# Graph attention layer on one core: score weights' products first, two load queues in the head, and 1/deviation moved into the transposes' matrix

## The chip, the cores and the metric

The kernel runs on one core of a Trainium2 chip. The metric is the device time of one execution in microseconds (us). Lower is better. Five engines work side by side, each through its own list of instructions in order: TensorE (PE, matmuls), VectorE (DVE), ScalarE (ACT), GpSimd (POOL) and SyncE (SP, which here only starts transfers). They wait for each other through semaphores.

## The reference

There are 2048 nodes with 256 features each. Cut to what matters:

```python
h0 = maximum(layernorm(x), 0.0)                      # (x - mean) / sqrt(var + 1e-5)
type_sum = adj @ h0
attn_a = sigmoid(concat([type_sum, h0]) @ Wa.T + ba)
attn_b = sigmoid(concat([type_sum, h0]) @ Wb.T + bb)
h = h0 @ W_sa
scores = (h @ a_left)[:, None] + (h @ a_right)[None, :]
e = where(adj != 0, exp(-leaky_relu(scores, 0.01)), 0.0)
x_a = (e / (e.sum(1, keepdims=True) + 1e-5)) @ h
x_b = adj @ (h0 @ W_gcnb) + b_gcnb
out = x + sigmoid(attn_a * x_a + attn_b * x_b)
```

`adj` is a 2048x2048 matrix of zeros and ones.

## The kernel before, in words

The nodes are 16 tiles of 128 (NT), taken in 8 pairs; the columns of the adjacency are four chunks of 512 (NC). Each float32 matrix is split into a high and a low float16 part (`_hi`, `_lo`), and a product is three matmuls: high by high, high by low, low by high.

The order of every engine is written out by hand. The work has these stages:

- **Head.** Units of one tile (0 and 1) or two tiles (2 to 8) go through `moments` (DVE: mean and variance), `norms` (POOL: 1/deviation by a power, `rstd`, then the shift), `h0_tiles` (ACT: the normalized, clipped tile in place in `x_sb`, counted by `h0_done`), `nat_highs` and `nat_lows` (the float16 parts of h0), `turn` (PE: transposes in float32 by the identity), `h0t_highs` and `h0t_lows` (the parts of the transposed tile) and `wide` (PE: h0 times the 260 wide columns, that is W_sa, two gate columns, and two score columns; the weights of the last two are products of W_sa and the attention vector, made at L926 from `c_sb`). Units 6 to 8 (tiles 10 to 15) are transposed by DMA instead (`turn_by_dma`, three times two transfers on SP's queue). `warm` runs matmuls on zeros.
- **b products** (`b_pair`, `b_products`, L822): h0 parts times the adjacency, chunk by chunk. Chunks 0, 1 and 2 come before the attention products of chunk 0, chunk 3 after those. Chunk 0 is interleaved with the head, pair by pair.
- **Attention** (`a_pair`, L863 to L865): DVE and ACT make `e` from the scores (`dve_z`, `act_exp`, `act_high`, `dve_low`), PE multiplies it by the weighted h. `post` (L856) applies the second weight matrix.

The scores of all nodes are needed as a row on every partition. `sl_lines` transposes them on PE, ACT copies them to `c_sb` (L388), SP stores them to memory (`sl_store`, L259) and loads them back broadcast (`sl_spread`, L264). This goes in three parts.

All loads of x and of the weights are on SP's queue. The adjacency is loaded by POOL (`load_adj`, L305) in 12 pieces, `ADJ_PIECES`: pieces 0 to 5 are chunk 0 (the first four with two tiles each), 6 and 7 chunk 1, 8 and 9 chunk 2. POOL starts piece 8 only when all six DMA transposes have landed (the loop at L337), and SP starts nothing out of its order. x is loaded in 7 parts, `X_PARTS`; below x5 is the part with tiles 8 to 11 and x6 that with tiles 12 to 15.

## Time and profile before

| | |
|---|---|
| time, median of 3 runs | 177.93 us (177.76 to 178.66) |
| the profiled execution, own time | 176.94 us |
| its span (first to last instruction) | 175.1 us |
| PE busy | 170.5 us, 97% of the span |
| DVE busy | 144.5 us, 83% |
| ACT busy | 113.2 us, 65% |
| POOL busy | 24.5 us, 14% |
| chain of work that ended last: PE's share | 97% |

The rows below come from that one execution; times within it count from the span's start. Outside the span lie 1.84 us of its own time. The busy time of PE includes the matmuls on zeros.

### The profile page before, as it was taken

The page shows a single profiled execution, that of the slowest core. Times are in us where ns is not written, and L with a number is a line of the kernel's source. Part 1 is how long each engine was busy: PE and PEld are TensorE (multiplying, and loading weights), DVE is VectorE, ACT ScalarE, POOL GpSimd, SP SyncE. Part 2 cuts the span into 40 slices and gives each one's busy share as a digit, 9 for nine tenths or more (in the row PEclk, how much of TensorE's full clock was granted, in tenths as well). Part 3 has the DMA queues.
Part 4 walks back from the last instruction along what each step waited for, and adds up shares of the span by engine and source line. Part 5 has one row for each costly group of instructions (what it writes and reads, how often), then busy time and mean ns, then how long its engine had stood idle before and what let it go on. Part 6 is the DMA issues. An engine that isn't in the chain of part 4 may idle for free.

```text
span 175.1 us, 3378 instructions
## 1 busy us (share of the span) xinstructions
PE 170.5 (97%) x1313; PEld 124.6 (71%) x1313; DVE 144.5 (83%) x306; ACT 113.2 (65%) x167; POOL 24.5 (14%) x43
## 2 busy tenths in 40 slices
PE   7999999999999999999999999999999999999992
PEld 2556764455554478888744488888888888888892
DVE  3799995589999995999999703999999999976551
ACT  3769996349868889298658600875875874863310
POOL 4846441002007930000000000000000000000000
PEclk9999999999999999999999999999999999999998
DMA  5999999986999369900010100000010010011101
GB/s 135 296 213 260 226 231 175 207 157 110 215 220 332 146 112 216 247 28 2 0 64 0 60 0 0 4 0 0 4 60 0 6 60 0 4 62 60 64 30 30
DMA packets 9071, 17.66 MB, mean 101 GB/s; under 512 B 3920, under 2 KB 4704, under 8 KB 8288
## 3 DMA queue, kind: packets, MB, share of 16 engines
q0 software_dynamic: 1728, 8.39, 25.0%
q1 hardware_dynamic: 7328, 9.06, 16.3%
q8 instruction: 10, 0.16, 0.4%
q14 instruction: 5, 0.04, 0.1%
HBM read 22.94 MB, written 2.11 MB: 143 GB/s over the span
## 4 chain that ended last, share of the span: by engine, by line
PE 97%; DVE 1%; issue 0%; ACT 0%; DVEq 0%
PE ps L822 32%; PE ps L865 16%; PE ps L863 16%; PE ps L864 16%; PE ps L856 6%; PE ps L797 6%; PE ps L905 3%; PE ps L791 1%; PE ps L926 0%; DVE logit L771 0%; DVE e_lo L557 0%; PE ps L818 0%; ACT logit L434 0%; DVE res L664 0%; DVE e_hi L519 0%
## 5 line engine op out<-in xcount | busy, mean ns | idle before, releaser
L863 PE MATMUL ps<-mv_lo,e_hi 128*128 128x257 f16 (+2 forms) x272 | 71.0, 267 | 0.0
L865 PE MATMUL ps<-mv_hi,e_lo 128*128 128x257 f16 (+2 forms) x272 | 70.9, 266 | 0.0
L864 PE MATMUL ps<-mv_hi,e_hi 128*128 128x257 f16 (+2 forms) x272 | 70.8, 266 | 0.0
L400 ACT ACTIVATE z<-z,log_e 128x1024 f32<-128x1024 f32 x32 | 36.7, 1146 | 31.2 <-DVE z L601 31.2
L601 DVE SCALAR_TENSOR_TENSOR z<-sl_row,exs,far 128x512 f32<-128x512 f32 x64 | 45.1, 746 | 0.6 <-DMA sl_row<-sl_line 0.6
L609 DVE TENSOR_TENSOR e_lo<-z,e_hi 128x1024 f16<-128x1024 f32 x32 | 39.0, 1220 | 1.4 <-ACT e_hi L410 1.4
L822 PE MATMUL ps<-adj,nat_lo 128*128 128x512 f16 x128 | 36.8, 379 | 0.0
L822 PE MATMUL ps<-adj,nat_hi 128*128 128x512 f16 x128 | 36.7, 379 | 0.0
L410 ACT ACTIVATE e_hi<-z 128x1024 f16<-128x1024 f32 x32 | 33.3, 1041 | 0.0
L863 PEld LDWEIGHTS ps<-mv_lo,e_hi 128*128 128x128 f16 x272 | 26.4, 97 | 3.4 <-ACT c_sb L388 0.3
L864 PEld LDWEIGHTS ps<-mv_hi,e_hi 128*128 128x128 f16 x272 | 26.5, 98 | 3.1
L865 PEld LDWEIGHTS ps<-mv_hi,e_lo 128*128 128x128 f16 x272 | 26.4, 97 | 3.1
L822 PEld LDWEIGHTS ps<-adj,nat_lo 128*128 128x128 f16 x128 | 12.5, 98 | 15.1
L822 PEld LDWEIGHTS ps<-adj,nat_hi 128*128 128x128 f16 x128 | 12.5, 98 | 13.1
L588 DVE TENSOR_SCALAR far<-adj 128x1024 f16<-128x1024 f16 x32 | 13.4, 421 | 0.2
L434 ACT ACTIVATE logit<-logit 128x512 f32<-128x512 f32 (+2 forms) x10 | 5.4, 537 | 9.3 <-DVE logit L651 5.3
L363 ACT ACTIVATE x_sb<-x_sb,shift,rstd 128x256 f32<-128x256 f32 x16 | 8.8, 590 | 3.3 <-POOL shift L312 3.3
L618 DVE SCALAR_TENSOR_TENSOR gate_in<-ps,gate_c 128x4 f32<-128x4 f32 x8 | 1.3, 157 | 10.5 <-PE ps L856 10.5
L305 POOL DMA_DIRECT2D adj<-in_adj_t x12 | 7.1, 591 | 16.0 <-DMA e_lo<-nat_lo 14.2
L856 PE MATMUL ps<-wg_hi,agg_hi 128*128 128x258 f16 x32 | 8.8, 274 | 0.0
L856 PE MATMUL ps<-wg_hi,agg_lo 128*128 128x258 f16 x32 | 8.7, 273 | 0.0
L856 PE MATMUL ps<-wg_lo,agg_hi 128*128 128x258 f16 x32 | 8.7, 272 | 0.0
(69 smaller groups left out, 170.0 us busy)
## 6 DMA issues: line engine op xcount, KB each, us to landing
adj<-in_adj_t POOLq DMA_DIRECT2D x6, 1024.0 KB, 9.8
x_sb<-in_x SPq DMA_DIRECT2D x6, 512.0 KB, 8.2
out<-res SPq DMA_DIRECT2D x7, 256.0 KB, 2.0
adj<-in_adj_t POOLq DMA_DIRECT2D x4, 256.0 KB, 6.7
adj<-in_adj_t POOLq DMA_DIRECT2D x2, 512.0 KB, 8.7
x_sb<-in_x SPq DMA_DIRECT2D x3, 256.0 KB, 4.0
sl_row<-sl_line SPq DMA_DIRECT2D x2, 256.0 KB, 5.5
sl_row<-sl_line SPq DMA_DIRECT2D x1, 512.0 KB, 7.0
```

The source lines that it names most:

```text
L363: act.activation(x_sb[:, t, :], x_sb[:, t, :], ACT.Relu, bias=shift[:, t:t + 1], scale=rstd[:, t:t + 1]).then_inc(h0_done, 1)
L400: act.activation(z[:, n % ZRING, :, :], z[:, n % ZRING, :, :], ACT.Exp, bias=log_e[:, 0:1], scale=SLOPE - 1.0).then_inc(exp_done, 1)
L410: act.activation(e_hi[:, s:s + 2, :], z[:, n % ZRING, :, :], ACT.Copy).then_inc(e_high, 1)
L588: dve.tensor_scalar(far[:, n % 2, :, :], adj16[:, c % ADJ, j:j + 2, :], -FAR, FAR, ALU.mult, ALU.add)\
L601: ins = dve.scalar_tensor_tensor(out=z[:, n % ZRING, u, :], in0=sl_row[:, c * CW:(c + 1) * CW], scalar=exs[:, j + u, SR:SR + 1], in1=far[: ...
L609: dve.tensor_tensor(e_lo[:, s:s + 2, :], z[:, n % ZRING, :, :], e_hi[:, s:s + 2, :], ALU.subtract)\
L797: ins = pe.matmul(ps[:, wide_bank(t), cols], h0t[a][:, t, k, :], wa2[b][:, k, cols], start=((a, b) == (0, 0) and k == 0), stop=(a == 1 and ...
L822: ins = pe.matmul(ps[:, B_BANKS[c] + k, :], nat[h][:, j, k * P:(k + 1) * P], adj16[:, c % ADJ, j, :], start=(j == 0 and h == 0), stop=(j = ...
L856: ins = pe.matmul(ps[:, 6 + q, 0:WG], agg[a][:, c % AGG, k, cols], wg2[b][:, k, :], start=(i == 0), stop=(i == len(three) - 1))
L863: pe.matmul(ps[:, bank, cols], e_hi[:, s, i1], mv_lo[:, j, cols], start=(j == 0), stop=False)
L864: pe.matmul(ps[:, bank, cols], e_hi[:, s, i1], mv_hi[:, j, cols], start=False, stop=False)
L865: return pe.matmul(ps[:, bank, cols], e_lo[:, s, i1], mv_hi[:, j, cols], start=False, stop=(j == NT - 1))
```

## The change

In PE's list the four small products of the score weights (L926 before, L1006 after) come ahead of all transposes. The first two tiles are only centred and clipped by ACT (`centred`), and their transposes become ordinary float32 matmuls whose second matrix is the identity times 1/deviation (`turn_scaled`, with `diagonal` on DVE); their float16 parts are scaled by `rstd` (`first_nat_highs`, `first_nat_lows`). The low parts of the first two tiles' wide products are put behind b products. Of matmuls on zeros, 12 become 6. `c_sb` and `wa_sb` are loaded from ACT's queue and no longer from SP's; `wg_sb` and `r_sb` are loaded after adjacency piece 8 has landed; x6 is started when x5 has landed; adjacency pieces 3 to 6 are each started behind one more unit's `norms`. From unit 4 on POOL makes two small operations that DVE made. ACT's order in the head is written out anew, with h0 halves ahead of evictions, and `wide` of units 3 to 5 comes later among the b products.

```diff
-WARM = 7
+WARM = 5
...
-SL_UNITS = (3, 5)
-SL_BANKS = (6, 6, 0)
+SL_UNIT = 3
+SL_BANKS = (6, 3, 0)
...
-WIDE_BANKS = (6, 2, 6, 2, 6, 2, 0, 2)
+
+POOL_FROM = 4
+
+NCENTRED = 2
+WIDE_BANKS = (6, 2, 6, 2, 0, 2, 0, 2)
...
+        diag = res[:, 0, :, 0:P]
...
-            sp.dma_start(wa_sb[:, :, :], w_wide).then_inc(wa_landed, 16)
-            sp.dma_start(c_sb[:, :], consts).then_inc(c_landed, 16)
             load_x(3)
             sp.wait_ge(x_landed[2], 16)
             load_x(4)
             sp.wait_ge(x_landed[3], 16)
             load_x(5)
-            sp.wait_ge(adj_landed[1], 16)
+            sp.wait_ge(x_landed[5], 16)
             load_x(6)
-            sp.wait_ge(x_landed[6], 16)
-            sp.dma_start(wg_sb[:, :, :], w_post).then_inc(wg_landed, 16)
-            sp.dma_start(r_sb[:, :], rows).then_inc(rows_landed, 16)
...
             sl_store(0)
+            sp.wait_ge(adj_landed[piece_of(1, 0)], 16)
             sl_spread(0)
-            sp.wait_ge(adj_landed[piece_of(0, NT - 1)], 16)
             turn_by_dma(ONTIME)
             turn_by_dma(ONTIME + 1)
             sl_store(1)
             turn_by_dma(ONTIME + 2)
             sl_spread(1)
             sp.wait_ge(adj_landed[piece_of(2, 0)], 16)
+            sp.dma_start(wg_sb[:, :, :], w_post).then_inc(wg_landed, 16)
+            sp.dma_start(r_sb[:, :], rows).then_inc(rows_landed, 16)
...
-                pool.wait_ge(var_ready, u + 1)
+                if u < POOL_FROM:
+                    pool.wait_ge(var_ready, u + 1)
+                else:
+                    pool.wait_ge(moments_done, UNITS[u][1])
+                    pool.tensor_scalar(var_s[:, ts], mean_var[:, ts, 1], LN_EPS, H_SCALE ** -2, ALU.add, ALU.mult).then_inc(var_ready, 1)
+                    pool.tensor_scalar(neg_mean[:, ts], mean_var[:, ts, 0], -1.0, None, ALU.mult).then_inc(neg_ready, 1)
+                    pool.wait_ge(var_ready, u + 1)
                 pool.tensor_tensor(rstd[:, ts], var_s[:, ts], power[:, 0:UNITS[u][1] - UNITS[u][0]], ALU.pow).then_inc(rstd_ready, 1)
+                if u < NCENTRED:
+                    return
                 pool.wait_ge(rstd_ready, u + 1)
+                if u >= POOL_FROM:
+                    pool.wait_ge(neg_ready, u + 1 - POOL_FROM)
+                if u < POOL_FROM:
+                    pool.wait_ge(centre_ready, u + 1)
                 pool.tensor_tensor(shift[:, ts], neg_mean[:, ts], rstd[:, ts], ALU.mult).then_inc(norm_ready, 1)
...
+            norms(3)
             load_adj(3)
-            norms(3)
+            norms(4)
             load_adj(4)
-            norms(4)
+            norms(5)
             load_adj(5)
-            norms(5)
+            norms(6)
             load_adj(6)
-            norms(6)
...
+            def centred(u):
+                act.wait_ge(centre_ready, u + 1)
+                act.activation(x_sb[:, u, :], x_sb[:, u, :], ACT.Relu, bias=neg_mean[:, u:u + 1], scale=1.0).then_inc(h0_done, 1)
+
             def h0_tiles(u):
...
+            def first_nat_highs():
+                act.wait_ge(h0_done, NCENTRED)
+                act.wait_ge(rstd_ready, NCENTRED)
+                for t in range(NCENTRED):
+                    ins = act.activation(nat_hi[:, t, :], x_sb[:, t, :], ACT.Copy, scale=rstd[:, t:t + 1])
+                ins.then_inc(nat_high, 1)
+
+            def w_wide_high():
+                act.wait_ge(wa_landed, 16)
+                act.activation(wa_hi[:, :, 0:WG], wa_sb[:, :, :], ACT.Copy, scale=W_SCALE).then_inc(wa_high, 1)
...
+            act.wait_ge(ident_ready, 1)
+            act.dma_start(c_sb[:, :], consts).then_inc(c_landed, 16)
+            act.dma_start(wa_sb[:, :, :], w_wide).then_inc(wa_landed, 16)
             act.wait_ge(consts_ready, 1)
             act.activation(table[:, :], log_e[:, :], ACT.Exp)
-            h0_tiles(0)
-            h0_tiles(1)
+            centred(0)
+            w_wide_high()
+            centred(1)
             h0t_highs(0)
+            first_nat_highs()
             h0t_highs(1)
             h0_tiles(2)
-            nat_highs(0)
             nat_highs(1)
             h0t_highs(2)
             h0_tiles(3)
+            nat_highs(2)
+            h0_tiles(4)
+            h0t_highs(3)
+            nat_highs(3)
             mv_highs(0)
-            nat_highs(2)
-            for p in range(1, NPAIR):
-                if p + 2 < NTURN:
-                    h0t_highs(p + 2)
-                if p + 2 < NPAIR:
-                    h0_tiles(p + 3)
-                    nat_highs(p + 2)
-                if p < ONTIME - 1:
-                    mv_highs(p)
-            mv_highs(ONTIME - 1)
+            mv_highs(1)
+            h0_tiles(5)
+            h0t_highs(4)
+            nat_highs(4)
+            h0_tiles(6)
+            nat_highs(5)
+            h0_tiles(7)
+            nat_highs(6)
+            h0t_highs(5)
+            mv_highs(2)
+            h0_tiles(8)
+            nat_highs(7)
+            mv_highs(3)
+            mv_highs(4)
             agg_highs(0)
-            act.wait_ge(wg_landed, 16)
-            act.activation(wg_hi[:, :, :], wg_sb[:, :, :], ACT.Copy, scale=W_SCALE).then_inc(wg_high, 1)
+            sl_lines(1)
...
+            def diagonal(u):
+                if u == 0:
+                    dve.wait_ge(ident_ready, 3)
+                dve.wait_ge(rstd_ready, u + 1)
+                dve.tensor_scalar(diag[:, u, :], ident[:, :], rstd[:, u:u + 1], None, ALU.mult).then_inc(diag_ready, 1)
+
+            def w_wide_low():
...
+            def turn_scaled(u):
+                pe.wait_ge(diag_ready, u + 1)
+                pe.wait_ge(h0_done, u + 1)
+                for k in range(KT):
+                    ins = pe.matmul(turn_bank(u)[:, 0, k, :], x_sb[:, u, k * P:(k + 1) * P], diag[:, u, :], start=True, stop=True)
+                ins.then_inc(turned, 1)
...
             warm(WARM)
-            pe.wait_ge(stats_done, 1)
-            warm(1)
-            pe.wait_ge(var_ready, 1)
-            warm(2)
-            pe.wait_ge(norm_ready, 1)
-            warm(1)
-            pe.wait_ge(ident_ready, 3)
-            turn(0)
-            warm(1)
-            turn(1)
-            pe.wait_ge(wa_high, 1)
-            pe.wait_ge(h0t_high, 1)
-            wide_part(0, slice(0, WG), ((0, 0),))
             pe.wait_ge(c_landed, 16)
             for k in range(KT):
                 for m in range(KT):
                     ins = pe.matmul(wl_bank[:, k, :], wt_sb[:, m, k * P:(k + 1) * P],
                                     c_sb[:, C_AVEC + 2 * m:C_AVEC + 2 * m + 2], start=(m == 0), stop=(m == KT - 1))
             ins.then_inc(wl_product, 1)
-            pe.wait_ge(wa_low, 1)
-            wide_part(0, slice(0, WG), ((0, 1),))
+            warm(1)
+            turn_scaled(0)
+            turn_scaled(1)
+            pe.wait_ge(wa_high, 1)
+            pe.wait_ge(wa_ready, 1)
+            for t in range(NCENTRED):
+                pe.wait_ge(h0t_high, t + 1)
+                wide_part(t, slice(0, WA), ((0, 0),))
+                pe.wait_ge(wa_low, 1)
+                wide_part(t, slice(0, WA), ((0, 1),))
+            b_pair(0)
+            turn(2)
             pe.wait_ge(h0t_ready, 1)
-            wide_part(0, slice(0, WG), ((1, 0),))
-            wide(1)
-            wide_part(0, slice(WG, WA)).then_inc(wide_product, 1)
-            turn(2)
-            b_pair(0)
-            for p in range(1, NPAIR):
-                b_pair(p)
-                if p + 2 < NTURN:
-                    turn(p + 2)
-                if p + 1 < NTURN:
-                    wide(p + 1)
-            b_products(1, 0, 8)
+            wide_part(0, slice(0, WA), ((1, 0),)).then_inc(wide_product, 1)
+            b_pair(1)
+            turn(3)
+            wide_part(1, slice(0, WA), ((1, 0),)).then_inc(wide_product, 1)
+            wide(2)
+            b_half_pair(2, 0)
+            turn(4)
+            b_half_pair(2, 1)
+            b_pair(3)
+            turn(5)
+            wide(3)
+            b_pair(4)
+            b_pair(5)
+            b_pair(6)
+            wide(4)
+            wide(5)
+            b_pair(7)
+            b_products(1, 0, 3)
+            pe.wait_ge(mv_ready, 8)
+            sl_lines(1)
+            b_products(1, 3, 8)
+            pe.wait_ge(sl_moved, 2)
             wide(6)
             b_products(1, 8, 12)
             pe.wait_ge(h0t_ready, NTURN)
```

The first place is PE's head, before the change (`e_hi` under 128x512 is the zeros tile, `c_sb` the score weights' products, `ident,x_sb` the transposes, `wa_*` the wide products, `adj,nat_*` the b products of chunk 0, from the first on):

```order
L905 MATMUL ps<-e_hi 128x512 x11
L791 MATMUL ps<-ident,x_sb 128x128 x2
L905 MATMUL ps<-e_hi 128x512
L791 MATMUL ps<-ident,x_sb 128x128 x2
L797 MATMUL ps<-wa_hi,e_hi 128x258 x2
L926 MATMUL ps<-c_sb 128x2 x4
L797 MATMUL ps<-wa_lo,e_hi 128x258 x2
L797 MATMUL ps<-wa_hi,e_lo 128x258 x2
L797 MATMUL ps<-wa_hi,e_hi 128x260 x2
L797 MATMUL ps<-wa_lo,e_hi 128x260 x2
L797 MATMUL ps<-wa_hi,e_lo 128x260 x2
L797 MATMUL ps<-wa_hi,e_hi 128x2 x2
```

and with the change (`res,x_sb` are the scaled transposes of the first two tiles):

```order
L998 MATMUL ps<-e_hi 128x512 x5
L1006 MATMUL ps<-c_sb 128x2 x4
L998 MATMUL ps<-e_hi 128x512
L882 MATMUL ps<-res,x_sb 128x128 x4
L888 MATMUL ps<-wa_hi,e_hi 128x260 x2
L888 MATMUL ps<-wa_lo,e_hi 128x260 x2
L888 MATMUL ps<-wa_hi,e_hi 128x260 x2
L888 MATMUL ps<-wa_lo,e_hi 128x260 x2
L911 MATMUL ps<-adj,nat_hi 128x512 x4
L911 MATMUL ps<-adj,nat_lo 128x512 x4
L875 MATMUL ps<-ident,x_sb 128x128 x4
L888 MATMUL ps<-wa_hi,e_lo 128x260 x2
```

The score weights' products moved from behind the first wide product to the front, and the b products of chunk 0 now start ahead of the third unit's transposes (the row under the b products) and of the first low products.

The second place is ACT around the first copy of the score lines (`c_sb<-ps 4x128`), before the change:

```order
L363 ACTIVATE x_sb<-x_sb,shift,rstd 128x256 x2
L373 ACTIVATE nat_hi<-x_sb 128x512
L379 ACTIVATE scale_a<-exs,log_s 128x2
L383 ACTIVATE mv_hi<-ps,scale_a 128x256 x2
L368 ACTIVATE e_hi<-ps 128x512
L363 ACTIVATE x_sb<-x_sb,shift,rstd 128x256 x2
L373 ACTIVATE nat_hi<-x_sb 128x512
L388 ACTIVATE c_sb<-ps 4x128
```

and with the change, from the evictions of the second pair's wide products on:

```order
L412 ACTIVATE scale_a<-exs,log_s 128x2
L416 ACTIVATE mv_hi<-ps,scale_a 128x256 x2
L385 ACTIVATE x_sb<-x_sb,shift,rstd 128x256 x2
L390 ACTIVATE e_hi<-ps 128x512
L406 ACTIVATE nat_hi<-x_sb 128x512
L385 ACTIVATE x_sb<-x_sb,shift,rstd 128x256 x2
L406 ACTIVATE nat_hi<-x_sb 128x512
L385 ACTIVATE x_sb<-x_sb,shift,rstd 128x256 x2
L406 ACTIVATE nat_hi<-x_sb 128x512
L390 ACTIVATE e_hi<-ps 128x512
L421 ACTIVATE c_sb<-ps 4x128
```

The copy stood behind the half of the fifth pair (the fifth `nat_hi` row of ACT), and stands now behind that of the seventh pair, which needs x6.

The third place is SP's queue up to the first DMA transpose, before the change:

```order
L239 DMA x_sb<-in_x 128x256 x2
L239 DMA x_sb<-in_x 128x512
L244 DMA wa_sb<-in_w_wide 128x516
L245 DMA c_sb<-in_consts 128x516
L239 DMA x_sb<-in_x 128x512 x2
L239 DMA x_sb<-in_x 128x1024 x2
L254 DMA wg_sb<-in_w_post 128x516
L255 DMA r_sb<-in_rows 128x258
L259 DMA sl_line<-c_sb 4x128
L264 DMA sl_row<-sl_line 128x512
L270 DMA_TRANSPOSE e_hi<-nat_hi 128x4x128
```

and with the change:

```order
L248 DMA x_sb<-in_x 128x256 x2
L248 DMA x_sb<-in_x 128x512 x3
L248 DMA x_sb<-in_x 128x1024 x2
L263 DMA sl_line<-c_sb 4x128
L268 DMA sl_row<-sl_line 128x512
L274 DMA_TRANSPOSE e_hi<-nat_hi 128x4x128
```

Four loads left the queue ahead of the store of the score lines (`sl_line`); its spread (`sl_row`) and the six transposes still follow it in order.

## Rows read from the trace of the kernel before

**Rows 1.** The page, part 2: 40 slices of 4.4 us; clock and DMA share in tenths.

```profile
PEclk9999999999999999999999999999999999999998
DMA  5999999986999369900010100000010010011101
```

**Rows 2.** Waits of PE over the whole span: total us, times, longest us.

```profile
PE ps L905 <- DVE e_hi L519: 1.2, 1, 1.2
PE ps L797 <- DVE e_lo L557: 0.3, 1, 0.3
```

**Rows 3.** Timeline of PE, 1 to 16 us: start us, length us, engine, line, operation, count.

```profile
1.18 4.88 PE L905 MATMUL ps<-e_hi 128*128 128x512 f16 x11 [1.18 <-DVE e_hi L519]
5.84 0.63 PE L791 MATMUL ps<-ident,x_sb 128*128 128x128 f32 x2
6.27 0.63 PE L905 MATMUL ps<-e_hi 128*128 128x512 f16 x1
...
7.26 0.95 PE L926 MATMUL ps<-c_sb 128*128 128x2 f32 x8
...
9.83 0.64 PE L791 MATMUL ps<-ident,x_sb 128*128 128x128 f32 x4
10.30 1.03 PE L822 MATMUL ps<-adj,nat_hi 128*128 128x512 f16 x4
...
14.42 0.38 PE L797 MATMUL ps<-wa_lo,e_hi 128*128 128x260 f16 x2
...
15.54 0.81 PE L822 MATMUL ps<-adj,nat_hi 128*128 128x512 f16 x3
```

**Rows 4.** Timeline of POOL and ACT, 3.9 to 5 us.

```profile
3.97 0.60 POOL L310 TENSOR_TENSOR rstd<-var_s,power 128x1 f32<-128x1 f32 x1
...
4.64 0.19 POOL L312 TENSOR_TENSOR shift<-neg_mean,rstd 128x1 f32<-128x1 f32 x1
...
4.87 0.60 ACT L363 ACTIVATE x_sb<-x_sb,shift,rstd 128x256 f32<-128x256 f32 x1 [2.65 <-POOL shift L312]
```

**Rows 5.** Line L305 from 3 to 5 us: adjacency piece 0, issue and us to landing.

```profile
L305 POOL DMA_DIRECT2D adj<-in_adj_t x1: 707/707/707, 3.2 to 3.2; - x1
...
DMA to landing us min/median/max: 5.5/5.5/5.5
```

**Rows 6.** Line L239 from 7 to 9 us: x5, issue and us to landing.

```profile
L239 SPq DMA_DIRECT2D x_sb<-in_x x1: 328/328/328, 7.1 to 7.1; - x1
...
DMA to landing us min/median/max: 7.4/7.4/7.4
```

**Rows 7.** Line L239 from 10 to 12 us: x6, issue and us to landing.

```profile
L239 SPq DMA_DIRECT2D x_sb<-in_x x1: 328/328/328, 10.7 to 10.7; - x1
...
DMA to landing us min/median/max: 8.7/8.7/8.7
```

**Rows 8.** Timeline, 21.7 to 26.5 us: unit 7's statistics and the seventh pair's high half.

```profile
21.81 0.74 DVE L527 BATCH_NORM_STATS2 stats<-x_sb 128x6 f32<-128x256 f32 x2
...
25.81 0.63 ACT L373 ACTIVATE nat_hi<-x_sb 128x512 f16<-128x512 f32 x1
```

**Rows 9.** Timeline of SP: the score lines' store and spread, first and last DMA transpose.

```profile
21.25 0.37 SPq L259 DMA_DIRECT2D sl_line<-c_sb  x1
27.99 0.35 SPq L264 DMA_DIRECT2D sl_row<-sl_line  x1
28.45 1.31 SPq L270 DMA_TRANSPOSE e_hi<-nat_hi  x1
...
37.20 2.15 SPq L270 DMA_TRANSPOSE e_lo<-nat_lo  x1
```

**Rows 10.** Line L305 at 41 us: adjacency piece 8, issue and us to landing.

```profile
L305 POOL DMA_DIRECT2D adj<-in_adj_t x1: 530/530/530, 41.0 to 41.0; - x1
...
DMA to landing us min/median/max: 7.5/7.5/7.5
```

**Rows 11.** Timeline of PE from 48.5 us: the first b products of chunk 2.

```profile
48.85 0.59 PE L822 MATMUL ps<-adj,nat_hi 128*128 128x512 f16 x2
```

129 lines of the change are left out of this document (81 added, 48 removed).

## The prediction

> **What bounds the kernel now.** I read the page first, then the waits, then the timelines of the places that the change touches. The list of PE's waits has two lines: 1.2 us before anything can start and 0.3 us in the head, for a low part of a transposed tile [rows 2]. From there to the end of its work PE never stands still, so a gain can only come from the head, before about 9 us, or from less work on PE. A loss can come from anywhere PE is made to wait. The page also shows what could make it wait: the DMA engines are full through the first eight slices, 0 to 35 us, while the clock row says full speed throughout [rows 1]. The clock row is not to be taken literally at the start: 11 matmuls of 512 columns on zeros took 4.88 us, 0.44 us each, which is 1.2 GHz, while from 10.30 us on four b products of 512 columns take 1.03 us with their overlapping tail, under 0.26 us each, which is 2.4 GHz [rows 3]. PE worked without a gap from 1.18 us until the clock had risen.
>
> **Accounting for the head.** I take the point at which the third b pair starts, 15.54 us before [rows 3]. From the first b product (10.30) to there PE does two b pairs, one set of transposes and one two-tile wide product: 5.24 us. With the change the same stretch holds two things more, because they now come behind the first b pair: the four transposes of unit 2 (9.83 to 10.30, 0.47 us [rows 3]) and the low products of tiles 0 and 1, four matmuls of 260 columns at 0.11 us (two start within 0.22 us at 14.42 [rows 3]), 0.45 us. With S for the new start of the first b pair, the third pair starts at S + 6.16. It is earlier than before only if S is below 9.38. The gain is 9.38 - S.
>
> **What sets S.** Removed: POOL's shift from the chain of the first tile. Before, `rstd` runs from 3.97 to 4.57, the shift from 4.64 to 4.83, ACT's tile starts at 4.87 and takes 0.60 us [rows 4], and the transposes follow at 5.84 [rows 3]. With the change ACT centres the tile while POOL makes the power, and DVE scales the identity afterwards. That operation is not in the trace; it costs between nothing and the 0.60 us of ACT's tile, which has twice the elements, and I take 0.2. The matrix is then ready near 4.9 instead of the tile at 5.5, if x lands as before. It will not quite: `c_sb` now travels beside x on ACT's queue, with twice its bytes and more; I allow 0 to 0.6 us of delay for x0 and take 0.4, my choice. So the first transposes start at about 5.3, half a us earlier. The four score weights' products (0.95 us as eight records [rows 3]) move into time in which PE ran zeros, which costs nothing. Dropping six matmuls on zeros costs nothing by itself either.
>
> ACT then has, in order, the halving of `wa_sb` (which must land first), the second tile's centring, one eviction of 256 columns, two scaled halves and a second eviction. At 0.4 to 0.6 us each (a tile takes 0.60 [rows 4], a two-tile half 0.63 [rows 8]) from about 5.5 this ends near 8.2, and the first b pair could start at 8.6 to 9.0. But adjacency piece 0 is not earlier: it is issued when x0 has landed (3.2 us) and takes 5.5 us, so 8.7 [rows 5], and with x0 0.3 to 0.4 later about 9.0. I take S = 9.2, bounds 8.4 and 10.0. The head gives 0.18 us, bounds +1.0 and -0.6.
>
> The scaled transposes are plain float32 matmuls of 128 columns, which the trace does not have. The nearest rows are the float32 products of two columns, 0.95 us for four, and the transposes, 0.43 us for two at the low clock (5.84 to 6.27) [rows 3]. I take 0.85 us for a tile's two, bounds 0.43 (no dearer than the transposes) and 1.9 (all four products' time twice). The page "TensorE: Matmul & The Clock Gate" of the Trainium skill, in its section "Terms", gives the transpose mode as four times faster for FP32, which speaks against this edit: it would make each pair of scaled transposes 1.7 us at the low clock. No run here shows it yet.
>
> **Clock.** The new list leaves gaps: after five matmuls on zeros PE is idle from 3.4 us (five at 0.44 from 1.18) until `c_sb` lands, which I put at 4.1,, and again around each scaled transpose. Before, it had none until the clock rose. If the rise comes after S, each us of real work until then costs half a us extra per us of time, so 0 to 1.3 us; I take 0.4.
>
> So PE comes to the first b product of chunk 2, 48.85 before [rows 11], at 48.85 - 0.18 + 0.4 = 49.1, if nothing in between stops it. POOL's ten added small operations are of the shift's kind, 0.19 us [rows 4], and take ten as small from DVE; they lie beside PE's work, and without that cover would cost 1.9 us.
>
> **What else gets later.** Moved weights first: `wg_sb` and `r_sb` no longer go ahead of the store of the score lines, and are needed by the first `post` only, amid the attention products of chunk 0. But x6 is started later. Before it was issued at 10.7 and landed 8.7 us later, 19.4 [rows 7], right behind x5, which landed at 14.5 (7.1 and 7.4) [rows 6]. Now it is issued when x5 has landed. I take x5 at 13.5, since adjacency piece 2 is started later and leaves room. From x5's landing x6 took 4.9 us although it was queued; unqueued it takes 4.9 to 8.7, I take 6.0: x6 at 19.5.
>
> From x6 the chain of unit 7 leads to the seventh pair's high half, from 21.81 (DVE) to 26.44 (end of ACT's half), 4.63 us before [rows 8]. ACT's copy of the score lines now stands behind this half and one eviction. With 0.6 and 0.25 for these, less 0.5 for time that ACT was merely busy, the store of the score lines is issued at 24.5; before it was at 21.25 [rows 9]. SP then waits for the store before it issues the spread: 6.74 us before (27.99), with two loads ahead [rows 9]. I take 4.5 now (bounds 3 and 6.7): the spread at 29.0. Behind it in SP's order are all six DMA transposes, the last issued at 37.20 for 2.15 us [rows 9], and behind them POOL's adjacency piece 8, issued at 41.0 and landing 7.5 us later, 48.5 [rows 10]. PE takes its first product from it at 48.85 [rows 11]. This is the thin place of the kernel: 0.3 us of slack. From spread to issue it was 13.0 us. The transposes' issues took 1.31 us at first and 2.15 at last; with the bulk loads done earlier I take 0.8 off: 12.2, bounds 10.5 and 13.0. Piece 8 is issued at 41.2 and lands at 48.8.
>
> **Sum.** The end moves by the later of the two, PE at 49.1 and the data at 48.8, against 48.85: +0.2 us. The own time of the profiled execution goes from 176.94 to 177.15. The median of the runs shown is 177.93, 0.99 above it, so I forecast 178.15 on that scale.
>
> The other rule that speaks against this is on the page "DMA: Bandwidth & Descriptors", section "Queues, rings and completion order" of the Trainium skill: each DMA engine takes turns between queues by packet. A second queue in the head then slows x0 rather than only adding a path, and small stores take turns with long adjacency packets. Here the first shows only as the allowance above.
>
> **The rivals.** (1) *The store chain decides, slower.* x6 at 20.3, the store at 25.3, 5 us to the spread, 12.7 and 7.5 us from there: piece 8 lands at 50.5, and PE waits. That is +1.65 us, 179.6 (own 178.6). It decides once piece 8 is issued after 41.3. For it: every step is in order on one queue and the slack was 0.3. Against it: `wg_sb` and `r_sb` are out of the way. Bound: x6 at 22.2, 6.7 and 13.0 give 54.4, +5.5; I do not believe all of them together. (2) *The clock rises late, slower.* Two us of real work behind S at 1.2 GHz: PE at 48.85 - 0.18 + 1.2, +1.0 us, 178.95. (3) *The head gains and nothing is lost behind.* S = 8.4 and a clock that has risen: -1.0 us, 176.95. It needs piece 0 before 8.4 and piece 8 before 47.9. Piece 0's 5.5 us speak against it. (4) *Scaled transposes at four times the transposes' time*, 4 x 0.43 = 1.7 us a tile at the low clock: the two tiles take 1.7 us more than I took, of which 0.9 lies beside ACT's work, so S is 10.0 and PE is busy enough for the clock: +0.6, 178.55, still no measurable change. This is what the page "TensorE: Matmul & The Clock Gate" of the Trainium skill would give. (5) The change doing nothing is inside my forecast: x0's delay cancels the earlier transposes.
>
> **How the numbers follow.** A measurement of this kernel can tell about 0.5%, 0.9 us. Forecast within 0.9 us: 0.40, and rival 4, 0.10, beside it: same 0.50. Rival 1 has 0.25 and rival 2 has 0.10: slower 0.35. Rival 3 has 0.15: faster. The forecast's own range is 177.2 to 178.8. The whole range goes down to rival 3, 176.9, and up past rival 1 to 180.2, which leaves out half of rival 3 and the tail of rival 1's bound.
>
> **What would show each step.** Right: the first b product at about 9.2; x0's statistics 0.3 to 0.5 later than before; piece 0 landing near 9.0; x6 landing at 19 to 20; the store of the score lines issued after 24; piece 8 issued near 41.2; PE without a wait above 0.3 us between 10 and 49 us. Wrong for the head: the first b product before 8.6 or after 10. Wrong for the chain: the store issued before 22, or PE waiting for an adjacency piece elsewhere, such as piece 1, 2 or 3, whose uses come 0 to 1.5 us earlier. Wrong altogether: PE waits in the middle of chunk 0 for x6's halves (it needs the seventh pair at S + 15.4 = 24.6, and 19.5 + 4.6 is 24.1), which would add up to 1 us ahead of the thin place and be hidden by rival 1 if that holds.

## The result and the profile after

The changed kernel takes 180.53 us (median of 22 runs, 178.21 to 184.20), the kernel before 177.31 us in the same sessions (22 runs, 176.62 to 178.66). The ratio is 1.011, 95% interval 1.008 to 1.014: slower, by less than 2%, with an interval clear of 1. This ratio and those below leave out every run more than 1.5% above the fastest of its kernel, which takes out ten of the changed kernel's 22 runs and none of the other's, while every median in us is over all runs (180.53 is 1.8% above 177.31). The spread grew as well.

The profiled execution of the changed kernel took 179.12 us (span 177.3), 2.2 more than that of before, and 1.4 less than its own median. What follows is read from it. First PE's waits over the whole span (total us, times, longest us), against two lines in [rows 2]:

```profile
PE ps L911 <- DMA adj<-in_adj_t: 1.5, 1, 1.5
PE ps L998 <- DVE e_hi L565: 1.2, 1, 1.2
PE ps L1006 <- DMA c_sb<-in_consts: 0.6, 1, 0.6
PE ps L911 <- DVE nat_lo L629: 0.2, 1, 0.2
```

There is a new wait for adjacency, and it has one place. PE's timeline around chunk 2's first b product, first a line of before (the product itself started at 48.85 [rows 11]), then of after:

```profile
48.62 0.38 PE L797 MATMUL ps<-wa_hi,e_lo 128*128 128x260 f16 x2
```

```profile
49.16 0.38 PE L888 MATMUL ps<-wa_hi,e_lo 128*128 128x260 f16 x2
51.04 0.59 PE L911 MATMUL ps<-adj,nat_hi 128*128 128x512 f16 x2 [1.50 <-DMA adj<-in_adj_t]
```

PE sat idle from 49.54 and started at 51.04, 2.19 us later than before, and its last product ends 2.19 us later too (174.15 against 171.96). So everything that was lost was lost before 51 us. The idle time tells a little less than the stop: records overlap, the next one started 0.23 us after such a row before (48.62 to 48.85), so without the wait the product would have started at about 49.39. The stop is 1.65 us, and every idle time below is about 0.15 short in the same way. The head (against [rows 3]):

```profile
1.18 2.32 PE L998 MATMUL ps<-e_hi 128*128 128x512 f16 x5 [1.18 <-DVE e_hi L565]
4.06 1.87 PE L1006 MATMUL ps<-c_sb 128*128 128x2 f32 x8 [0.56 <-DMA c_sb<-in_consts]
...
6.17 1.96 PE L882 MATMUL ps<-res,x_sb 128*128 128x128 f32 x8
7.91 0.64 PE L888 MATMUL ps<-wa_hi,e_hi 128*128 128x260 f16 x2
...
9.48 1.02 PE L911 MATMUL ps<-adj,nat_hi 128*128 128x512 f16 x4
10.35 1.03 PE L911 MATMUL ps<-adj,nat_lo 128*128 128x512 f16 x4
11.21 0.60 PE L875 MATMUL ps<-ident,x_sb 128*128 128x128 f32 x4
11.64 0.39 PE L888 MATMUL ps<-wa_hi,e_lo 128*128 128x260 f16 x2
11.87 1.02 PE L911 MATMUL ps<-adj,nat_hi 128*128 128x512 f16 x4
13.06 1.04 PE L911 MATMUL ps<-adj,nat_lo 128*128 128x512 f16 x4 [0.17 <-DVE nat_lo L629]
...
14.37 0.39 PE L888 MATMUL ps<-wa_hi,e_lo 128*128 128x260 f16 x2
```

The first b product is at 9.48, 0.82 us earlier than before, but the score weights' products alone now take 1.87 us where they took 0.95: PE runs at 1.2 GHz until 9.29 (until 6.91 before, and the 0.95 came after it). And PE's work from the first b product to chunk 2, busy time over those stretches, first of before, then of after (window, length, busy, matmul records, granted clock, DMA share, GB/s):

```profile
10.30:48.85 38.55, 38.55 (x229) 1.00 0.95 198
```

```profile
9.48:49.54 40.06, 39.89 (x236) 1.00 0.96 179
```

The busy time grew by 1.34 us, but not all of that is moved work. The rows that moved behind the first b product are unit 2's transposes (11.21 to 11.64, 0.43 us) and the two pairs of low products (0.23 us each, 11.64 to 11.87 and again at 14.37): 0.89 us. The rest is the two stops, whose first 0.15 us count as busy, and 0.13 us by which unit 5's transposes at 19.83 last longer than the other sets. So the head alone is about even, and the waits are the loss: -0.82 + 0.89 (moved work) + 0.13 + 0.33 (the low half at 13.06, a stop of 0.33 us by the distance of the starts) + 1.65 (piece 8) = 2.18 of the 2.19 us.

Where piece 8 was held is told by the chain that ended last, from 17 to 52 us in order of time (start us, us, what):

```profile
19.86 10.90 DMA adj<-in_adj_t
30.76 0.02 issue
30.78 0.35 SPq L268
...
31.17 2.30 SPq L274
...
39.35 2.98 DMA e_lo<-nat_lo
...
42.36 0.04 POOLq L356
42.41 0.49 issue
42.90 8.00 DMA adj<-in_adj_t
50.90 0.14 issue
51.04 1.02 PE ps L911 x4
```

Piece 6 of the adjacency lands at 30.76, that releases the spread of the score lines (27.99 before [rows 9]), behind it go the six DMA transposes, the last lands at 42.34, and that releases piece 8 (42.90; 41.0 before [rows 10]). ScalarE's timeline and SP's waits show a second thing at the same gate:

```profile
23.73 0.63 ACT L406 ACTIVATE nat_hi<-x_sb 128x512 f16<-128x512 f32 x1
24.27 0.58 ACT L390 ACTIVATE e_hi<-ps 128x512 f16<-128x512 f32 x1
24.74 0.25 ACT L421 ACTIVATE c_sb<-ps 4x128 f32<-4x128 f32 x1
```

```profile
SPq L266 <- DMA sl_line<-c_sb: 3.9, 1, 3.9
...
SPq L268 <- DMA adj<-in_adj_t: 1.5, 1, 1.5
```

The score lines are copied at 24.74, stored at 25.02, and the store has landed at about 29.3 (25.35 + 3.9); only then comes the wait for piece 6. So the spread has two late releasers, 1.5 us apart. In the kernel before, piece 6 (issued at 17.39) landed at 28.22, only 0.23 us after the spread at 27.99: the new wait costs this much because POOL also issues the piece 2.5 us later.

### The profile page after: what moved, and what is told of

Same layout as the page of the kernel before. It is cut to its first block, busy times and chain, and to the rows that moved or that the text cites. A ratio compares the mean times of both kernels' runs of the same rounds, so it can differ in the third digit from the quotient of the medians.

```text
span 177.3 us, 3373 instructions
## 1 busy us (share of the span) xinstructions
PE 170.7 (96%) x1305; PEld 125.6 (71%) x1305; DVE 143.7 (81%) x298; ACT 113.9 (64%) x169; POOL 27.2 (15%) x51
## 3 DMA queue, kind: packets, MB, share of 16 engines
q0 software_dynamic: 1728, 8.39, 25.2%
## 4 chain that ended last, share of the span: by engine, by line
PE 74%; DMA 14%; SPq 5%; POOL 2%; ACT 1%; DVE 1%; issue 1%; POOLq 0%; DVEq 0%
PE ps L911 17%; PE ps L957 16%; PE ps L958 16%; PE ps L956 16%; DMA adj<-in_adj_t 11%; PE ps L949 6%; SPq L274 4%; DMA c_sb<-in_consts 2%; DMA e_lo<-nat_lo 2%; PE ps L1006 1%; PE ps L882 1%; PE ps L888 1%; POOL rstd L322 1%; ACT x_sb L385 1%; POOL shift L330 0%
## 5 line engine op out<-in xcount | busy, mean ns | idle before, releaser
L957 PEld LDWEIGHTS ps<-mv_hi,e_hi 128*128 128x128 f16 x272 | 26.5, 98 | 3.2
L956 PEld LDWEIGHTS ps<-mv_lo,e_hi 128*128 128x128 f16 x272 | 26.4, 97 | 3.3
L958 PEld LDWEIGHTS ps<-mv_hi,e_lo 128*128 128x128 f16 x272 | 26.4, 97 | 3.1
L685 DVE SCALAR_TENSOR_TENSOR gate_in<-ps,gate_c 128x4 f32<-128x4 f32 x8 | 1.3, 157 | 11.2 <-PE ps L949 11.2
L311 POOL DMA_DIRECT2D adj<-in_adj_t x12 | 7.3, 608 | 19.4 <-DMA e_lo<-nat_lo 17.2
L570 DVE BATCH_NORM_STATS2 stats<-x_sb 128x6 f32<-128x256 f32 x16 | 6.2, 417 | 3.0 <-DMA x_sb<-in_x 2.9
## 6 DMA issues: line engine op xcount, KB each, us to landing
adj<-in_adj_t POOLq DMA_DIRECT2D x6, 1024.0 KB, 10.8
```

Of the source, the lines that this page charges most:

```text
L311: pool.dma_start(adj16[:, c % ADJ, lo:hi, :], adj_t[c, :, lo:hi, :]).then_inc(adj_landed[i], 16)
L956: pe.matmul(ps[:, bank, cols], e_hi[:, s, i1], mv_lo[:, j, cols], start=(j == 0), stop=False)
L957: pe.matmul(ps[:, bank, cols], e_hi[:, s, i1], mv_hi[:, j, cols], start=False, stop=False)
L958: return pe.matmul(ps[:, bank, cols], e_lo[:, s, i1], mv_hi[:, j, cols], start=False, stop=(j == NT - 1))
```

## Experiments

Ratios are to the kernel before, measured beside each, with 95% intervals. Times within a run come from one profiled execution of each kernel, which can lie anywhere among its runs: those of e2 and e3 are the fastest and the second fastest of twelve (177.41 and 177.33 us), those of e4 and e5 the slowest of twelve (181.31 and 181.74). Line numbers in the experiments are off by one or two from the changed kernel's.

**e1: the old gate.** Piece 5 is waited for, behind the spread, instead of piece 6 ahead of it.

```diff
             sl_store(0)
-            sp.wait_ge(adj_landed[piece_of(1, 0)], 16)
             sl_spread(0)
+            sp.wait_ge(adj_landed[piece_of(0, NT - 1)], 16)
```

> The changed kernel, only that SP waits for adjacency piece 5, as before the change, and not for piece 6, and does so behind the spread of the score lines instead of ahead of it. Theory A (the new gate on piece 6 decides when the queue behind it starts): the spread is issued at 29.3 us, when the store has landed, instead of 30.8; piece 8 lands at 49.4 instead of 50.9, PE waits for it 0.1 us or less instead of 1.5, and the time falls by 1.4 us against the changed kernel, to within 0.9 us of the kernel before. Rival B (the loads' bandwidth decides, not the gate): the spread goes out earlier but the transposes wait behind piece 7, piece 8 lands within 0.4 us of 50.9 and the time stays. Rival C (the late store decides, behind x6's half on ACT): the store lands only at 30.5 or later in most runs and less than 0.4 us comes back.

Measured: 1.015 (1.010 to 1.021), 180.58 us. The store went at 25.80, the spread at 31.32 when the store had landed, piece 8 at 44.43 to 52.08, and PE waited 2.36 us. The gate alone is not the cause: the store steps into its place. In this profile the clock rose only at 10.81, after the first b product (9.72), and the b products before it started 0.43 us apart instead of 0.22: about 0.5 us.

**e2: POOL's old order.** Pieces 3 to 6 are issued one unit's norms earlier, as before.

```diff
-            norms(3)
             load_adj(3)
-            norms(4)
+            norms(3)
             load_adj(4)
...
```

> The changed kernel with POOL's loads of adjacency pieces 3 to 6 each one unit's norms earlier, as before the change; the gate on piece 6 stays. Theory A (piece 6 is late because POOL issues it late, at 19.9 us instead of 17.4): piece 6 is issued near 17.8 and lands 10.9 us later, near 28.7; the spread then waits for the store, 29.3; piece 8 lands near 49.4 and the time falls by 1.3 to 1.5 us. Rival B (piece 6 is late because the DMA engines are full): issued earlier, it lands after 30 all the same and the time falls by less than 0.4 us. Rival D: earlier adjacency packets slow x5 and x6, the store goes out after 26 us, and the time rises by 0.5 us or more.

Measured: 1.006 (1.002 to 1.010), 179.33 us. Piece 6 was issued at 17.36 and landed at 26.82. Now the store alone holds the spread (25.17, spread 30.39); piece 8 lands at 49.19, and PE waits 0.31 us at 49.33, all in the fastest of its twelve runs. The ratio is about half of the changed kernel's loss, but the two intervals overlap.

**e3: seven products on zeros** (`WARM = 7`).

> The changed kernel with seven matmuls on zeros at its start instead of five, so that PE has no gap before the score weights' products. If piece 8 decides the end alone, the time stays within 0.3 us, whatever the head does. In the trace the clock should rise earlier than 9.3 us (near 7), the first b product should start at 9.0 to 9.2 instead of 9.48, and PE should come to chunk 2 about 0.5 us earlier and wait for piece 8 that much longer (2.0 instead of 1.5 us). The rival is that the head still decides in part: then 0.5 us come back in the time.

Measured: 1.005 (0.999 to 1.010), 179.96 us. In the profile the clock rose at 5.09 and b began at 8.39. PE then waited 0.94 us at 18.11 for piece 3 and came to chunk 2 at 49.25: 1.1 us were gained at the start, and most of it was waited away. What I had not expected: it did not wait for piece 8 at all. With both releasers as in the changed kernel, piece 6 landed at 29.03, the spread went at 29.37 and piece 8 landed at 48.94. So the lateness of that chain is not the same in every execution.

**e4: the loads alone.** The kernel before, with the change's gates, POOL's order, x6 behind x5 and the late `wg_sb` and `r_sb`, and its own head.

```diff
-            sp.wait_ge(adj_landed[1], 16)
+            sp.wait_ge(x_landed[5], 16)
             load_x(6)
-            sp.wait_ge(x_landed[6], 16)
-            sp.dma_start(wg_sb[:, :, :], w_post).then_inc(wg_landed, 16)
...
             sl_store(0)
+            sp.wait_ge(adj_landed[piece_of(1, 0)], 16)
             sl_spread(0)
-            sp.wait_ge(adj_landed[piece_of(0, NT - 1)], 16)
...
```

> The kernel before with the change's load order behind the head alone: SP's gate on piece 6, x6 started when x5 has landed, the post weights loaded after piece 8 and split later, POOL's pieces 3 to 6 each one unit later. Head, ACT's order and the two queues are as before. Theory A: the gate on piece 6 works here too; piece 6 lands near 30.5, the spread goes out then instead of 28.0, piece 8 lands near 50.7 and the time rises by 1.5 to 2.2 us against the kernel before, nearly all of the change's loss. Rival C (ACT's copy behind the seventh half is needed for the loss): the time rises by less than 0.7 us. A further possibility is that PE also waits for x6's halves in chunk 0, which would show as waits before 30 us and not add to the end.

Measured: 1.007 (1.003 to 1.011), 178.89 us. The store left at 19.94, and still the spread waited for piece 6 (issued 20.48, landed 29.86); piece 8 went at 43.08, PE waited 2.62 us. Here piece 6 alone holds the spread, with the store landed long before. The edit has POOL's later issue in it as well, and no run takes the two apart in the old head. This profile is the slowest of its runs, and 1.7 us of it are the clock's (last section).

**e5: the copy early.** ScalarE's copy of the score lines right behind `h0t_highs(4)`. The same edit is in e6 to e9 and in e12.

```diff
-SL_BANKS = (6, 3, 0)
+SL_BANKS = (7, 3, 0)
...
-                if p + 1 == SL_UNIT:
-                    sl_lines(0)
...
             h0t_highs(4)
+            sl_lines(0)
...
-                        pe.wait_ge(mv_ready, t - 3)
+                        pe.wait_ge(mv_ready, max(t - 3, 2))
...
+                    if t == 5:
+                        pe.wait_ge(sl_moved, 1)
```

> The changed kernel, with ScalarE's copy of the first score lines out of PSUM taken right behind h0t_highs(4) instead of inside mv_highs(2) (and in bank 7, so that nothing has to be waited for). Copy at about 20.6 us instead of 24.7, so the store is issued at about 21.1. Theory A (the spread is released by the later of the store's landing and piece 6's landing): piece 6 still lands at 30 to 31 us, so nothing is won: spread at 30 to 31, piece 8 issued at 42 to 43, a wait of 0.8 to 1.8 us before chunk 2, ratio to the kernel before 1.005 to 1.012. Rival B (the store alone decides): spread at 26 to 27, piece 8 lands before 48, no wait, ratio 0.998 to 1.003.

Measured: 1.010 (1.006 to 1.013), 179.89 us. The gate decides: piece 6 landed at 32.79, spread at 32.80, piece 8 at 45.57, PE waited 1.40 us there (in its slowest run, with piece 6 issued 2.5 us later than in the changed kernel's profile). Something else came in: 2.5 us of waiting for piece 1 at 14.75.

**e6: early copy and old gate** (e5 with e1).

> The changed kernel with the early copy and the old gate (spread first, then a wait for piece 5). Theory A: the store is issued at 21.1 and lands at 25.5 to 27, piece 5 has landed at 23, so the spread goes at 25.5 to 27, the six transposes behind it end early enough that piece 8 is issued at 38 to 40.5 and lands by 48; TensorE, arriving at about 49.3, does not wait. Span 175.3 to 176.0, ratio 0.998 to 1.004. Rival C (the head itself, and not the wait, lost the time: clock rise at 9.3 instead of 6.9): no wait and still 1.005 or more. Rival D (the piece-8 chain is bound by piece 7 and POOL's queue, not by the spread): piece 8 issued at 41 or later in spite of a spread at 26.

Measured: 1.008 (1.004 to 1.011), 179.37 us. The store went at 21.40 and the spread at 26.80, four us earlier than in the changed kernel, but piece 8 at 42.85, as late as there. PE waited 0.59 us for piece 3 and 0.63 for piece 8. This is rival D's sign. The six transposes start earlier and end no earlier: from the first one's issue to the last one's landing they took 15.0 us here, 11.2 in the changed kernel and 12.0 before; the second's issue alone took 4.40 us, while piece 7 was in flight. In all the profiles the first transpose landed 0.5 to 2.3 us after piece 7, although it was issued anywhere from 26.4 to 33.2. That piece 7 holds them is likely by this, and no run tests it.

**e7: early copy and POOL's old order** (e5 with e2).

> The changed kernel with the early copy and POOL's loads in the order of before (each piece of 3 to 6 one unit's norms earlier), gate on piece 6 kept. Theory A: piece 6 is issued at 17.4 and lands at 27 to 28.5, which is later than the store (about 26), so the spread goes at 27 to 28.5 as in the kernel before (27.99), piece 8 is issued at 39.5 to 41.2 and lands at 47.5 to 49; wait before chunk 2 none or up to 0.3. Ratio 0.998 to 1.005. Rival C (head lost the time): 1.005 or more without a wait.

Measured: 1.008 (1.005 to 1.012), 179.36 us. The spread went at 27.93, as before, and piece 8 landed at 49.90, before PE asked. PE's waits between 10 and 60 us:

```profile
PE ps L912 <- DMA adj<-in_adj_t: 0.6, 1, 0.6
PE ps L912 <- ACT nat_hi L406: 0.3, 1, 0.3
```

The wait before chunk 2 is gone and the kernel is still 0.8% slower. The reading by that wait alone falls here: PE stops elsewhere. Nor was the chain to piece 8 mended. It landed 1.3 us later than before (48.56), and without its other stops PE would have been there at about 49.1, 0.8 us ahead of it.

**e8: all of these, and seven products on zeros** (e1, e2, e3 and e5 together).

> The changed kernel with the early copy, the old gate, POOL's loads in the old order, and 7 products on zeros instead of 5. Theory A: the chain to piece 8 is early by 1 us or more, and the clock rises at about 5.1 (as it did in the kernel with 7 products), first product of b at 8.4 instead of 9.2 (before: 10.30). TensorE then arrives at chunk 2 at 48.0 to 48.9 and piece 8 has landed at 47.5 to 48.5. Span 174.3 to 175.3, ratio 0.993 to 1.000: the first of these kernels that may beat the kernel before. Rival E (what the head gains is given back at the pieces of adjacency, of which piece 3 then comes too late, by 0.9 us): ratio 0.999 to 1.003, with a wait at piece 3 and first product at 8.4. Rival C: 1.005 or more.

Measured: 1.003 (1.000 to 1.006), 178.30 us, the best of the twelve. The seven products on zeros did not raise the clock early this time: it rose at 9.18 (5.09 in e3), and b began at 9.54. In the profile PE waits after the head for one thing, piece 1. PE's timeline, then line L311 (POOL's adjacency loads) from 6 to 7 us:

```profile
11.70 0.39 PE L887 MATMUL ps<-wa_hi,e_lo 128*128 128x260 f16 x2
13.80 0.38 PE L912 MATMUL ps<-adj,nat_hi 128*128 128x512 f16 x1 [1.72 <-DMA adj<-in_adj_t]
```

```profile
L311 POOL DMA_DIRECT2D adj<-in_adj_t x1: 592/592/592, 6.3 to 6.3; - x1
...
DMA to landing us min/median/max: 7.4/7.4/7.4
```

Piece 1 holds tiles 2 and 3, which is the second b pair. In the kernel before that pair started right behind the first:

```profile
12.03 1.03 PE L822 MATMUL ps<-adj,nat_hi 128*128 128x512 f16 x4
```

So the old head asked for piece 1 at 12.03, when it had been there since 10.7 (issued 5.6, 5.1 us to landing): 1.3 us to spare. The new one asks at 11.0 to 12.7, hardly earlier, but piece 1, issued at 6.1 to 6.4, lands between 10.5 and 14.6. The expectation of e9 has 3.7 us here, from 15.54, which is the third pair and wants piece 2; that is a misreading of mine. Piece 8 landed at 49.64, and without the wait for piece 1 PE would have asked for it at about 49.0.

**e9: x5 held** (e8, with x5 behind piece 0's landing instead of x3's).

```diff
-            sp.wait_ge(x_landed[3], 16)
+            sp.wait_ge(adj_landed[0], 16)
             load_x(5)
```

> The last kernel (early copy, old gate, POOL's old order, 7 products on zeros) with x5 sent behind piece 0's landing (about 8.1 us) instead of behind x3's (6.5). Theory F (in the changed head TensorE asks for piece 1 at 11.8 us, 3.7 us earlier than before, and piece 1, issued at 6.1 to 6.3, lands between 11.7 and 14.6 because x4 and x5 are in flight with it): with x5 held, piece 1 lands by 11.8, no wait there, chunk 2 is reached at 48.6 to 49.2, and ratio 0.994 to 1.001. Rival G (piece 1 is late by x4 and the weights alone): piece 1 still lands at 12.5 to 14, wait of 0.5 to 1.7 there, ratio 1.001 to 1.006. Rival H: x5 is late for its statistics (it would land at 14.5 to 16) and a later pair waits for it.

Measured: 1.014 (1.009 to 1.018), 179.82 us. Piece 1 landed at 10.62, as theory F has it, the clock rose at 4.32, b began at 8.22, and PE paid later on. Its waits from 10 to 50 us:

```profile
PE ps L912 <- DMA adj<-in_adj_t: 1.4, 1, 1.4
PE ps L912 <- DVE nat_lo L628: 1.2, 1, 1.2
PE ps L912 <- ACT nat_hi L406: 0.5, 1, 0.5
```

The first is piece 2 (9.07 to 16.19, beside x5 from 8.00 to 14.32); the others are halves behind x6, which waits for x5 and landed at 22.71. Rival H came in kind, with x6 in the place of x5. What one load gains another loses.

**e10: piece 8 early** (the changed kernel, with piece 8 released by the fourth DMA transpose).

```diff
-            for p in range(ONTIME, NPAIR):
+            for p in range(ONTIME, NPAIR - 1):
                 pool.wait_ge(h0t_landed[p - ONTIME], 32)
             load_adj(8)
+            pool.wait_ge(h0t_landed[NPAIR - 1 - ONTIME], 32)
```

> The changed kernel with one difference: POOL issues piece 8 when the first four transposes by DMA have landed instead of all six (its slot has been free from the start; only the order was held by hand). In the changed kernel the fourth landed at 38.73 and the sixth at 42.34, so piece 8 goes at about 39.3 instead of 42.90 and lands at 47 to 49.5. Theory A (the wait before chunk 2 is a part of the loss, and the head the other): the 1.5 us of waiting go to 0 to 0.3, TensorE reaches chunk 2 at about 49.5, ratio 1.002 to 1.006, 0.5 to 0.8% better than the changed kernel. Rival C (the head alone): the wait goes, and the ratio stays at 1.008 or more. Rival I (the fifth and sixth transpose now come too late for the last wide products, needed at 48.0): a wait at the last wide products in its place, ratio unchanged at 1.009 to 1.012.

Measured: 1.013 (1.009 to 1.018), 179.74 us. The copy was late in this profile (store 27.50, spread 32.58), so piece 8 went at 42.48 all the same and landed at 50.88; PE did not wait for it only because piece 1 (landed 13.56) had already cost it 1.75 us at 13.70.

**e11: the head alone** (the changed kernel with the later loads as before: e1, e2, x6 behind piece 1, `wg_sb` and `r_sb` early; `c_sb` and `wa_sb` stay on ACT's queue).

> The changed kernel with the loads as before (x6 behind piece 1, POOL's pieces 3 to 6 before the norms, spread ahead of the wait for piece 5, wg and rows early): the head's products, its two queues and the lists of ScalarE and VectorE alone. Theory A: the store is still issued at 24.5 to 25.5 and decides: spread at 29.5 to 31, piece 8 lands at 49.2 to 51.5, wait 0.3 to 2. Together with the head (arrival at 49.0 to 49.6): ratio 1.004 to 1.010, near the kernel with POOL's old order (1.006). Rival J (the two parts of the change only hurt together): 0.998 to 1.002. Rival K (the early weights and rows, which cross piece 6, make the store's landing later still): 1.010 or more.

Measured: 1.006 (1.001 to 1.010), 179.14 us. Store 26.04, spread 30.88, piece 8 at 43.52 to 51.91, a wait of 2.22 us before chunk 2 and 0.25 us at piece 1. The two parts of the change, each alone, cost 0.7% (e4) and 0.6% (here), together 1.1%.

**e12: e8 with piece 8 early** (e10's edit).

> All that helped, together: the changed kernel with the early copy of the score lines, the old gate, POOL's loads in the old order, 7 products on zeros, x5 where the change put it, and piece 8 released by the fourth transpose. The profiles so far give chunk 2's arrival as the start of b plus 39.4 to 39.9 us plus the waits for pieces on the way. Theory L (the head is bound by the DMA engines, which are busy from 2 us on: what is asked for earlier is waited for): start of b at 8.3 to 9.7, piece 1 at 11.5 to 13.8 against a demand at 11.0 to 11.9, piece 8 lands at 46 to 48, no wait there; chunk 2 reached at 48.9 to 50.9, ratio 1.000 to 1.006, that is, no better than the kernel before even with the wait before chunk 2 gone for certain. Theory A (the wait before chunk 2 was the main loss): ratio 0.994 to 1.000.

Measured: 1.011 (1.006 to 1.016), 180.02 us. Piece 8 went at 40.16, took 10.8 us beside the last transposes and landed no earlier than in the changed kernel, at 50.92. PE waited 1.53 us for piece 1 and 0.94 us for halves of `nat`, ran at half the clock from 7.26 to 10.68, and reached chunk 2 at 52.30. It gave up what e8 had.

**The ledger of the profiles.** First b product, chunk 2's first, PE's waits between them, and what is left, then two landings and the execution's own time (us; the waits are the idle times in PE's timeline, those under 0.1 us left out). e4 has the old head:

```
kernel        first b   chunk 2   waits   rest    piece 1   piece 8   own time
before         10.30     48.85    0.00    38.55    10.70     48.56     176.94
after           9.48     51.04    1.67    39.89    11.69     50.90     179.12
e1              9.72     52.21    2.36    40.13    12.15     52.08     180.27
e2              9.33     49.33    0.31    39.69    11.68     49.19     177.41
e3              8.39     49.25    0.94    39.92    10.51     48.94     177.33
e4              9.93     51.54    2.74    38.87    10.88     51.40     181.31
e5              9.70     53.63    4.04    39.89    14.61     53.50     181.74
e6              9.61     50.58    1.22    39.75    10.85     50.44     179.06
e7              9.65     50.52    0.88    39.99    12.85     49.90     178.57
e8              9.54     50.84    1.72    39.58    13.67     49.64     178.92
e9              8.22     51.72    3.18    40.32    10.62     50.95     179.81
e10             9.40     51.01    1.75    39.86    13.56     50.88     179.07
e11             9.70     52.05    2.47    39.88    12.50     51.91     180.10
e12             9.13     52.30    2.47    40.70    13.84     50.92     180.37
```

Two things can be read from it. Own time less the arrival at chunk 2 is 128.1 us in every row but e6 (128.5) and e4 (129.8, the clock): what differs between these kernels happens before chunk 2. And the rest, less about 0.15 us for each wait, is 39.4 to 39.8 us with the new head in most rows and 38.6 with the old one; what is above that is PE at half the clock (e1, e12) or stops too short to be listed (e9). The lowest, 39.4, is the old head's 38.55 and the 0.89 us of moved work. So to arrive when the old head arrives, b must start at about 9.4 and PE must not stop. The changed kernel's 9.48 is nearly that; where it starts much earlier (e3, e9) the data are not there.

## Why the prediction was right or wrong

The range held (1.011 times 177.93 is 179.9; the medians of all runs would give 181.2, above it), the likeliest case did not. What came is rival 1's, slower through the chain to piece 8, with its size (179.6) but in part by luck: x6, which it had at 20.3, landed at 17.86, and the spread was released by a gate that it does not name. By steps:

- **Right, the head.** Forecast 9.2 for the first b product, measured 9.48, and break-even at 9.38, measured about 9.4. x0's delay of 0.4: piece 0, issued on x0's landing, went at 3.68 instead of 3.2 [rows 5]. `c_sb` landed at 4.01 (4.1). Moved work behind the start: 0.92, measured 0.89. The 0.4 for the clock did not come there, since the clock rose at 9.29, before the first b product; what the low clock cost lies ahead of it. In e1 it did come, about 0.5 us with a rise at 10.81: rival 2 in small. Piece 0 was a miss that cost nothing (8.07 instead of 9.0, it was not last). Of the 0.28 us by which S was late, the score weights' 1.87 us at 1.2 GHz carry the most: my row for them, 0.95 us at 7.26, stood in the old profile after the clock's rise at 6.91, and I called them free. Rival 3, the head gaining a whole us, was seen in the profiles of e3 and e9 (8.39, 8.22); neither came to chunk 2 before 48.85.
- **Right, the scaled transposes.** From 6.17 to 7.91 PE does two tiles: 0.87 us each at the low clock, where I took 0.85. The transposes by identity took 0.43 for a tile's two blocks at the same clock [rows 3], so the plain float32 product costs twice, not four times as much. By the four times in "TensorE: Matmul & The Clock Gate", section "Terms", of the Trainium skill a tile would have taken 1.7, an estimate; the trace does not agree, and rival 4 falls.
- **Wrong, the spread of the score lines at 29.0.** Measured 30.78. The prediction had one releaser, the store, at 24.5 plus 4.5 us. The store was nearly right (25.02, landed about 29.3, which is 4.3 us for 4.5). What it left out is the gate that the diff puts in front of the spread: piece 6, which POOL now issues at 19.86 and which takes 10.9 us. The line of the diff was on record and was never priced: a term put at nothing without a reason, and 1.5 us beyond the store's landing. e4, where the store leaves at 19.94 and the spread still goes at 29.87, shows that piece 6, issued late and waited for, suffices without a late store; e1, that without the gate the store takes over.
- **Right in size, wrong in cause, the store at 24.5.** I derived it from x6 landing at 19.5. x6 landed at 17.86, and the copy was as late as I said, because ScalarE's list puts it behind two halves and an eviction, and ScalarE worked without a stop from 14.89 up to the copy at 24.74. e5 to e9 and e12, where the copy stands earlier in that list, store at 21.25 to 23.40.
- **Right, from spread to piece 8.** 12.2 forecast, 12.12 measured; then 8.0 us to landing instead of 7.6. The miss of 2.1 us in piece 8's landing (50.90 for 48.8) is 0.5 for the store's issue, 1.3 for the spread behind it (0.2 less for the store's landing and 1.5 more for the gate), -0.1 and 0.4.
- **Left out, when piece 1 lands.** I had named it as a sign against me by its use, "0 to 1.5 us earlier", and that holds (11.87 for 12.03). What had no term is its landing, 11.69 for 10.70: it is issued 0.5 us later, as x0 and piece 0 are, and takes 5.6 us for 5.1. The margin went from 1.3 us to 0.18 us in the changed kernel's own profile; in six other profiles of this head PE waited 0.25 to 2.5 us for it.

What is shown: both parts of the change slow the kernel by themselves (e4, e11); the spread has two releasers, and removing one leaves the other (e1, e2, e5). With both out of the way (e6, e7, e8) the spread goes at 26.8 to 27.9 and the kernel is still 0.3 to 0.8% slower: piece 8 lands at 49.64 to 50.44, 1.1 to 1.9 us later than before, and PE also stops for piece 1 or piece 3. That e7 and e8 show no wait before chunk 2 is due in part to those earlier stops. The engines for DMA are full from about 2 us on (share 0.96 from 9.48 to 49.54), so an earlier demand meets the same bytes.

What stays open: what holds the six transposes when the spread is early (piece 7 is the candidate, untested), and how often the unprofiled runs lose time at piece 1, at piece 8 or to the clock. The changed kernel's median lies 1.4 us above its profile. Its sixteen runs with a mean granted clock of 0.997 or more have a median of 179.57; the other six, at 0.989 to 0.991, took 182.12 to 184.20. The sessions ran on different chips, and the changed kernel itself was not run again beside e5 to e12, so differences of 0.3% among those say little. No version beat the kernel before.

## What to carry to other kernels

Where the DMA engines are full, starting the consumer earlier gains nothing unless its data were early too: before pulling work forward, list when each piece will land and when it would be asked for, and count what work moves behind the start. A landing can move while the demand stays, as piece 1's did. A transfer with two conditions in front of it is released by the later one; price every wait that the diff adds, above all one for a transfer that the same diff delays, before pricing the one you find interesting. And a margin of 0.3 us at the end of a chain through three queues is none.
